# A fused attention and gated feed-forward kernel: idle matmuls at the start, kept products ahead of a rotary sum, and a split last projection

## What is computed

```python
xn = _layernorm(x, axis=-1)
# attention
q, k, v = xn @ wq, xn @ wk, xn @ wv          # heads of 128
q, k = _rope(q, pos), _rope(k, pos)
scores = einsum('bqhgd,bshd->bhgqs', qg, k) * sm_scale
allowed = (j <= i) & (j > i - SLIDING_WINDOW)
attn = softmax(where(allowed, scores, neg), axis=-1)
s = einsum('bhgqs,bshd->bqhgd', attn, v).reshape(...) @ wo
# feed-forward, W1, W2, W3 dequantised from 4 bits with a scale per 64
h = silu(xn @ W1.T) * (xn @ W3.T)
g = _silu(h @ W2.T)
x = x + s * g
```

## Time and profile before

| what | value |
|---|---|
| median of 3 runs | 816.35 us (815.01 to 816.83) |
| the profiled execution, its own time | 816.31 us |
| its span | 814.5 us |
| TensorE (PE) busy | 799.0 us, 98% of the span |
| VectorE (DVE) busy | 564.8 us, 69% |
| ScalarE (ACT) busy | 428.2 us, 53% |
| GpSimd (POOL) busy | 484.3 us, 59% |
| TensorE in the chain that ended last | 75% |
| GpSimd in the chain that ended last | 15% |

### The profile page before, as it was taken

How to read it: one execution, slowest core, us unless ns; L and a number is a source line. 1 busy time by engine, 2 the same in 40 slices (tenths; PEclk the granted TensorE clock), 3 DMA queues, 4 the chain that set the end, 5 groups by cost and what they waited for, 6 DMA issues and landing times.

```text
span 814.5 us, 13389 instructions
## 1 busy us (share of the span) xinstructions
PE 799.0 (98%) x3928; PEld 668.5 (82%) x3928; DVE 564.8 (69%) x1628; ACT 428.2 (53%) x1103; POOL 484.3 (59%) x362
## 2 busy tenths in 40 slices
PE   6999999999999999999999999999999999999987
PEld 4888888888888888888888888888888888888876
DVE  6625858576558867767686777768677676867774
ACT  4412313223138675666656576665656666665562
POOL 2112324224156774877488497747839774789985
PEclk9999999999999999999999999999999999999999
DMA  9449525211000400400030040003004001220102
GB/s 286 147 164 271 157 78 139 82 39 52 0 28 14 130 14 0 131 1 14 12 118 13 0 129 0 13 28 101 13 0 129 0 13 38 91 64 0 39 1 104
DMA packets 51908, 54.00 MB, mean 66 GB/s; under 512 B 4128, under 2 KB 33184, under 8 KB 51872
## 3 DMA queue, kind: packets, MB, share of 16 engines
q1 hardware_dynamic: 51584, 53.49, 22.0%
q10 hardware_dynamic: 288, 0.07, 0.0%
HBM read 47.25 MB, written 6.29 MB: 66 GB/s over the span
## 4 chain that ended last, share of the span: by engine, by line
PE 75%; POOL 15%; issue 6%; DVE 1%; ACT 1%; DMA 0%; POOLq 0%; ACTq 0%; DVEq 0%
PE bank L1270 20%; PE bank L1271 20%; PE bank L1272 20%; POOL wol L398 5%; POOL swap L424 5%; PE bank L1384 2%; PE bank L1397 2%; PE bank L1311 2%; PE bank L1316 2%; PE bank L1322 2%; POOL q L428 2%; POOL pl L447 1%; POOL ph L447 1%; POOL acc L455 1%; PE bank L1414 1%
## 5 line engine op out<-in xcount | busy, mean ns | idle before, releaser
L424 POOL TENSOR_TENSOR swap<-swap,cst 128x512 f32<-128x512 f32 x80 | 108.4, 1355 | 39.6 <-ACT swap L665 39.6
L686 ACT ACTIVATE probs<-probs,nmx 128x128 f32<-128x128 f32 x256 | 100.0, 392 | 60.4 <-DVE nmx L1055 60.4
L1270 PE MATMUL bank<-xh,wih 128*128 128x512 f32 x320 | 128.9, 403 | 0.0
L1271 PE MATMUL bank<-xl,wih 128*128 128x512 f32 x320 | 125.2, 391 | 0.0
L1272 PE MATMUL bank<-xh,wil 128*128 128x512 f32 x320 | 125.0, 391 | 0.0
L1270 PE MATMUL bank<-woh,oh 128*128 128x512 f32 x256 | 100.5, 392 | 0.1
L1271 PE MATMUL bank<-wol,oh 128*128 128x512 f32 x256 | 100.2, 391 | 0.0
L1272 PE MATMUL bank<-woh,ol 128*128 128x512 f32 x256 | 99.9, 390 | 0.0
L374 POOL TENSOR_TENSOR hl<-act_h,hh 128x512 fp32r<-128x512 f32 x22 | 32.0, 1454 | 102.2 <-ACT hh L564 102.2
L428 POOL TENSOR_TENSOR q<-q,swap 128x512 f32<-128x512 f32 x64 | 85.5, 1335 | 6.7 <-DVE q L1030 1.8
L447 POOL TENSOR_TENSOR ph<-ph,cst 128x512 fp32r<-128x512 f32 x32 | 42.8, 1338 | 72.0 <-ACT ph L701 72.0
(11 more groups left out here) (121 smaller groups left out, 2006.5 us busy)
## 6 DMA issues: line engine op xcount, KB each, us to landing
raw<-in_wq SPq DMA_DIRECT2D x32, 256.0 KB, 5.0
raw<-in_wo SPq DMA_DIRECT2D x32, 256.0 KB, 4.9
pk<-in_w SPq DMA_DIRECT2D x44, 128.0 KB, 3.7
sc<-in_s SPq DMA_DIRECT2D x44, 128.0 KB, 3.9
vals<-stage SPq DMA_DIRECT2D x16, 256.0 KB, 2.5
vraw<-vals SPq DMA_DIRECT2D x16, 256.0 KB, 3.0
pk<-in_w SPq DMA_DIRECT2D x11, 256.0 KB, 2.7
sc<-in_s SPq DMA_DIRECT2D x11, 256.0 KB, 3.0
```

The lines of the kernel that those rows point to most:

```text
L424: nc.gpsimd.tensor_tensor(v, v, spread(sin.unsqueeze(1), P, 2, SEQ), ALU.mult).then_inc(sin_done, 1)
L686: e = nc.scalar.activation(probs[:, s, c0:c1], probs[:, s, c0:c1], ACT.Exp, bias=nmx[:, s, i:i + 1], scale=-1.0, accum_out=rsum[:, s, i:i ...
L1270: nc.tensor.matmul(out_, sh, mh, start=(i == 0), stop=False)
L1271: nc.tensor.matmul(out_, sh, ml, start=False, stop=False)
```

## The change

1. **Start, TensorE.** `keep_busy(13)`: 13 matmuls on a zeroed tile `idle` (set by GpSimd) run ahead of the wait for the identity and the first turn; `keep_busy(2)` follows the first turn. Their bank is not read.
2. **Start, value units.** Of the waits in `v_unit` only those that can still be open are kept. Unit 0 does its four low-token matmuls ahead of the turn of tile 1, which stood between the first and the second four; with half 0 the low weights are taken in the order 0, 1, 3, 2.
3. **Start, GpSimd and VectorE.** GpSimd makes five chunks of `wvl` and VectorE three; GpSimd's waits are now on `ln_small` 6 and 12, the end of the small steps of tiles 0 and 1, and no longer on the normalised tiles.
4. **Feed-forward.** W2 tile 9 is handled beside tile 9 and no longer beside tile 10 (`W2_AT`), on all three engines. The first scores wait for the reading of token tile 7 alone; the wait for tile 6 stands ahead of the second scores.
5. **Attention steps.** On GpSimd `sin_part` is cut into product and sum, and the kept products of block 1 stand between product and sum of chunk 3. On ScalarE `p_hi(…, 1, 1)` stands ahead of `kq_hi(…, 2)`, and on VectorE `p_lo(…, 1, 1)` ahead of `kq_lo(…, 2)`.
6. **Last group.** `rest_product` 4 and 5 move from between the rotary parts to behind them.
7. **End.** The last out-projection is 24 matmuls of 256 columns, first the left half of the columns into O_B[1], then the right half into S_B[0], each with its own count; `finish_last` takes the halves as they come.

```diff
+        W2_AT = [()] + [(t - 1,) for t in range(1, FT - 2)] + [(FT - 3, FT - 2), (FT - 1,)]
...
-            pool.wait_ge(xn_here, 1)
-            wv_lo(0)
-            pool.wait_ge(xn_here, 2)
-            wv_lo(1)
-            wv_lo(2)
+            nc.gpsimd.memset(idle[:, :], 0.0).then_inc(idle_set, 1)
+            pool.wait_ge(ln_small, 6)
+            wv_lo(0, 0)
+            wv_lo(0, 1)
+            pool.wait_ge(ln_small, 12)
+            wv_lo(0, 2)
+            wv_lo(1, 0)
+            wv_lo(1, 1)
...
-                if last:
-                    rest_product(4)
                 sin_part(ng, nbp, 1)
-                if last:
-                    rest_product(5)
                 sin_part(ng, nbp, 2)
-                sin_part(ng, nbp, 3)
+                sin_product(ng, nbp, 3)
                 near(g, bp, 1)
+                sin_sum(ng, nbp, 3)
                 sin_part(ng, nbp, 4)
                 if last:
-                    rest_product(6)
-                    rest_product(7)
+                    for t in range(4, NT):
+                        rest_product(t)
                     for t in range(4, NT):
                         rest_sum(t)
...
                 p_hi(g, bp, 1, 0)
+                p_hi(g, bp, 1, 1)
                 kq_hi(ng, nbp, 2)
-                p_hi(g, bp, 1, 1)
                 halves(ng, nbp, 4)
                 kq_hi(ng, nbp, 3)
                 o_hi(g, bp, 2)
...
-                pe.wait_ge(xh_done, i + 1)
+                if half == 0:
+                    pe.wait_ge(xh_done, i + 1)
                 for d in range(DT):
-                    pe.wait_ge(wvh_done, DT * half + d + 1)
+                    if n in (0, 2):
+                        pe.wait_ge(wvh_done, DT * half + d + 1)
                     nc.tensor.matmul(out_, xh[:, d, cols], wvh[:, half, d, :], start=(d == 0), stop=False)
-                if ahead:
+                if ahead and n:
                     ahead()
...
+                if ahead and not n:
+                    ahead()
+                for d in ((0, 1, 3, 2) if half == 0 else range(DT)):
...
+            def keep_busy(n):
+
+                for _ in range(n):
+                    nc.tensor.matmul(bank[5][:, 0:P], idle[:, :], idle[:, :], start=True, stop=True)
...
+            pe.wait_ge(idle_set, 1)
+            keep_busy(13)
             pe.wait_ge(id_in, 16)
             x_turn(0)
+            keep_busy(2)
...
+            def last_project():
+
+                pe.wait_ge(ol_done, cnt(4, NKV - 1, 1, 4))
+                pe.wait_ge(acc_done, cnt(4, NKV - 1, 1, 2))
+                pe.wait_ge(masked, cnt(8, NKV - 1, 1, 7))
+                for half in range(2):
+                    cols = slice(half * D // 2, (half + 1) * D // 2)
+                    three(last_bank[half][:, cols], [(oh[:, 3, h, :], ol[:, 3, h, :], woh[:, h, cols], wol[:, h, cols])
+                                                 for h in range(GH)]).then_inc(y_ps, 1)
```

More of the change, by code:

```diff
@@ L94, in build @@
         warm = sb("warm", [P, 4], f32, ffn)
+        idle = sb("idle", [P, P], f32, ffn)
         stat = sb("stat", [P, NT, 6], f32, ffn)
@@ L186, in build @@
         PARTS = ((0,), (1,), (2, 3), (4, 5, 6, 7))
+        FIRST_LOW = ((0, 0), (0, 1), (0, 2), (1, 0), (1, 1))
+        THEN_LOW = ((0, 3), (1, 2), (1, 3))
         HERE = (0, 1, 2, 4, 6)
@@ L410, in _ @@
                 hid_lo(t, 0)
[L411 to L414, removed]
+                for u in W2_AT[t]:
+                    w2_lo(u)
                 hid_lo(t, 1)
@@ L428, in sin_part @@
                 nc.gpsimd.tensor_tensor(dst, dst, swap[:, s, :], ALU.add).then_inc(rope_done, 1)
+            def sin_part(g, bp, c):
+                sin_product(g, bp, c)
+                sin_sum(g, bp, c)
             pool.wait_ge(const_in, 16)
@@ L641, in _ @@
                         act.wait_ge(v_kept[i], 16 * (VU // 4))
[L642 to L645, removed]
+                for u in W2_AT[t]:
+                    w2_hi(u)
                 silu(t, 1)
@@ L967, in _ @@
             x_lo(1)
-            for d in range(DT):
-                wv_lo(1, d)
+            wv_lo(1, 2)
+            wv_lo(1, 3)
             stats(2)
@@ L1005, in _ @@
                     dequant13(t + 2, 1)
[L1006 to L1009, removed]
+                for u in W2_AT[t]:
+                    dequant2(u)
                 hid(t, 1)
@@ L1113, in finish_last @@
                 n = NT - 1
-                dve.wait_ge(y_ps, cnt(4, NKV - 1, 1, 4))
                 dve.wait_ge(rest_done, NT)
                 for half in range(2):
+                    dve.wait_ge(y_ps, cnt(4, NKV - 1, 1, 4 + half))
                     cols = slice(half * D // 2, (half + 1) * D // 2)
-                    nc.vector.tensor_tensor(gate[:, n, cols], O_B[1][:, cols], gate[:, n, cols], ALU.mult) \
+                    nc.vector.tensor_tensor(gate[:, n, cols], last_bank[half][:, cols], gate[:, n, cols], ALU.mult) \
                         .then_inc(acc_done, 1)
@@ L1222, in step @@
                 p_lo(g, bp, 1, 0)
+                p_lo(g, bp, 1, 1)
                 kq_lo(ng, nbp, 2)
-                p_lo(g, bp, 1, 1)
                 masking(ng, nbp, 0, 0, 1)
@@ L1307, in v_unit @@
                 out_, cols = bank[2 + n % 4][:, :], slice(i * P, (i + 1) * P)
-                pe.wait_ge(xh_done, i + 1)
+                if half == 0:
+                    pe.wait_ge(xh_done, i + 1)
                 for d in range(DT):
-                    pe.wait_ge(wvh_done, DT * half + d + 1)
+                    if n in (0, 2):
+                        pe.wait_ge(wvh_done, DT * half + d + 1)
                     nc.tensor.matmul(out_, xh[:, d, cols], wvh[:, half, d, :], start=(d == 0), stop=False)
-                if ahead:
+                if ahead and n:
                     ahead()
-                pe.wait_ge(xl_done, i + 1)
+                if half == 0:
+                    pe.wait_ge(xl_done, i + 1)
                 for d in range(DT):
                     nc.tensor.matmul(out_, xl[:, d, cols], wvh[:, half, d, :], start=False, stop=False)
[L1317 to L1322, removed]
+                if ahead and not n:
+                    ahead()
+                for d in ((0, 1, 3, 2) if half == 0 else range(DT)):
+                    if n in (0, 2) and (half, d) in FIRST_LOW:
+                        pe.wait_ge(wvl_first, FIRST_LOW.index((half, d)) + 1)
+                    elif n in (0, 2):
+                        pe.wait_ge(wvl_done, THEN_LOW.index((half, d)) + 1)
+                    m = nc.tensor.matmul(out_, xh[:, d, cols], wvl[:, half, d, :], start=False,
+                                         stop=(d == (3 if half else 2)))
                 m.then_inc(vu_ps, 1)
+            def keep_busy(n):
+                for _ in range(n):
+                    nc.tensor.matmul(bank[5][:, 0:P], idle[:, :], idle[:, :], start=True, stop=True)
             def w13_tile(t):
@@ L1450, in _ @@
             w2_mult(FT // 2, (0,), (7, 6, 4))
+            pe.wait_ge(ffn_read, place(FT // 2, 7))
+            scores(0, 0, 0, 0)
             pe.wait_ge(ffn_read, place(FT // 2, 6))
-            scores(0, 0, 0, 0)
             scores(0, 0, 0, 1)
@@ L1496, in step @@
                     out_project(g, bp, 2)
-                    out_project(g, bp, 3)
+                    last_project()
                     return
```

18 lines of the change are left out of this document (11 added, 7 removed).

## The result

The changed kernel takes **839.63 us** (median; 837.79 to 840.53, 4 runs) where the kernel before takes 816.59 (815.01 to 817.72, 4 runs) beside it: ratio 1.0279, 95% interval 1.0259 to 1.0299. It is slower, as forecast, but by 23 us and not by 16, and 0.6 us above the range of 825 to 839. The profiled execution took 840.53 with a span of 838.7.

What follows compares the result with a forecast made beforehand. TensorE, busy 799.0 of 814.5 us, was taken as the bound. Terms 21.8 - 2.3 - 2.2 - 0.3 - 0.3 - 0.6 = +16.1 us on 816.31 gave 832.4 us, range 825 to 839.

Steps and rivals of the forecast that it cites:

- The chain: Full attention steps: sum 4 behind both kept products delays `kq_hi`, `o_hi`, `o_lo`; TensorE's `out_project` 1 at 6.93, not 5.03.
- The sum of the gaps: 13 full steps: 1.90 us each in seven with bp=1, 1.41 in six with bp=0, together +21.8 us.
- the first step of the last group: Rest products behind the rotary parts shorten its 9.30 us distance to some 7.6; -2.3 us in all, bounds 0 and -4.5.
- the 0.6 for `finish`: Last group: VectorE's `finish` ahead of `p_lo` delays the chain by about 0.6, so 6.93 becomes some 7.6.
- Start, W2 and first scores: Unit 1 starts at 11.9, not 14.06 (-2.2); the `W2l` wait goes (-0.3); first scores wait for tile 7 alone (-0.3).
- The end: Last projection in halves: only one half's product and sum follow TensorE; -0.6 us, bounds 0 and -0.9.
- Rival 1: Whole kernel gets faster, because the held `o_hi` does not hold TensorE; about 806 us, chance 0.09.
- Rival 3: Gap smaller: GpSimd or ScalarE runs its chain part tighter, or only one step kind pays; 821 us, chance 0.07.
- rival 2: Attention steps: the clock falls at every new gap; chance 0.05.
- the part on what would show it: Signs in the profile: 13 `ol` waits of about 1.9 us, distance 6.9, unit 1 near 11.9, granted clock 1.00 through the steps.
- behind the gap their distances stay as they are: Attention steps: other engines shift along with TensorE, so the gaps add up in full and nothing more is lost.
- `p_hi` and `p_lo` earlier: Block 1 of attention steps: `ph` starts no earlier, and `kq_hi` of chunk 2 comes 0.6 us later; effect nothing.

Runs made afterwards that it cites:

- experiment 1: Changed kernel with ScalarE's `kq_hi` of chunk 3 moved behind the two `o_hi` of the step: 813.32 us, against 816.34 for the kernel before.
- Experiment 3: Kernel before with only GpSimd's kept products put between product and sum of chunk 3: 838.42 us, ratio 1.0269 to the kernel before.
- the kernel with the gap filled: Changed kernel with 8 unread matmuls of 512 columns ahead of `out_project` 1 in every full step: 834.37 us.
- experiment 6: Changed kernel with VectorE's list alone put back, `p_lo(…, 1, 1)` behind `kq_lo` of chunk 2: 850.78 us.

## Where the prediction was wrong, and where it was right

The step that failed is a term that I put at nothing: the falls of the clock behind the new gaps. The runs show 5.3 us in its place, and two smaller costs, of 1.4 and 0.7 us, that were not in the sum either. The chain that makes the gaps was right.

**Right: the mechanism and its place.** The chain turn, `ph`, two kept products, sum, `kq_hi`, `o_hi`, `o_lo` is what the trace shows, and experiment 1 cuts it at the link named. The steps of the working, from the turn: kept product 1.32 (1.31 measured), sum 3.82 (4.00), `kq_hi` 5.15 (5.32), `o_hi` 5.47 (5.64), `o_lo` 6.09 (6.25), TensorE 6.93 (7.00). The 0.18 lost at `pl` is partly given back by a shorter handover at the end. The sum of the gaps was +21.8 and is +22.5 (13.7 + 8.8), the 0.7.

**Right in size, partly by luck:** the first step of the last group, -2.3. Its distance alone gives 2.3, since it is 7.0 and not 7.6 (the 0.6 for `finish` did not come), and the last step has 0.45 more, where the kernel before still ran at the low clock (0.50 in 780.00 to 781.00, 0.77 in the next microsecond). The -2.3 has a 0.6 in it for matmuls at the low clock; no run shows that term by itself, and the trace of before shows 0.75 in its place: the matmul at L1423 takes 0.80 and the one of `out_project` 1 0.63, against 0.50 and 0.40 in the earlier trace rows, and from the one to the other it is 1.66 us (778.63 to 780.29) against 0.91 (634.14 to 635.05). Start, W2 and first scores were -2.8 together (-3.1 in the trace); unit 1 at 11.97 against the forecast 11.9 is a lucky hit, since eight other traces with this start have 12.22 to 12.82, and the start alone measured 1.3. The end, -0.6 (-0.65 in the trace, not resolved by itself). Rival 1, the faster one, needed the sum to be no hindrance; it is excluded. Rival 3 is excluded too.

**Wrong, and the step that failed: rival 2 was priced as all or nothing.** I wrote of the clock falling "at every new gap", gave it 0.05, and put nothing of it into the forecast, with the ground that each new gap stands alone, while ahead of the 0.52 of the earlier trace rows three stood close together. In the trace of before these are the 0.49 of the earlier trace rows and

```profile
775.73 0.47 PE L1414 MATMUL bank<-ph,vh 128*128 128x512 f32 x1 [1.15 <-DVE pl L1077]
...
777.39 0.51 PE L1420 MATMUL bank<-ph,vh 128*128 128x512 f32 x1 [0.73 <-POOL ph L447]
```

The new gaps do stand alone (those that end at 617.91 and 655.15 are 37 us apart), and the clock fell behind four of the 14 all the same, at 1.57 us each. The low stretch of the earlier trace rows had cost 1.3: the 0.75 above and 0.53 from `out_project` 1 to `out_project` 2 (4.45 us, where the step of the earlier trace rows has 3.92). So a price was at hand, a little low, and the count was wrong. By the kernel with the gap filled it is 5.3 us of the 7.2 between forecast and result. The granted clock was not at 1.00 through the steps, as the part on what would show it had expected. The rival's own sign of being right, a clock near 0.5 in windows behind the gaps, came at four of them.

**Wrong: "behind the gap their distances stay as they are".** After a wait the second matmul comes 0.11 later than in a running row (0.34 against 0.23): +1.4 over 14 stretches, in the fourth row of the table. One of the 14 lies behind `first_step`, where the same loss follows a hold of only 0.18 us at the weight load.

**Wrong: `p_hi` and `p_lo` earlier cost "nothing".** They move VectorE's `ql` into the start of GpSimd's `pl`. I had this as an upper bound of the gap, 2.3, but not as a cost of this edit. Experiment 3 puts it at 0.17 to 0.19 each step; it is inside the 7.00, where shorter handovers hide most of it.

Without the falls the forecast of 832.4 stands against 834.4 measured: 1.4 behind the waits and 0.7 in the gaps.

**Wrong: the upper end of the range.** By the bounds that I gave, 832.4 + 5.2 + 2.5 is 840.1, and I wrote 839. The result lies below 840.1, but this would have been luck: that room was meant for slower kept products, and the falls filled it.

**Open:** why the clock falls behind some gaps and not behind others of the same length. The earlier W2 tile, the first scores' wait and the rest products were seen in the traces but not run by themselves.

## What to carry to other kernels

When an instruction moves back on one in-order engine, ask which instruction on the next engine waits for it, and what stands queued behind that one, though it needs nothing of it: here 0.15 us of slack two engines further decided 29 us. A wait of 0.5 us in every other step was worth removing, but by filling idle time earlier on the late engine, not by overtaking something that others wait for. And price a new repeated gap in TensorE's row with a share of falls of the clock (here 4 behind 14 gaps of 1.8 us), with the cost of one taken from the trace (here 1.57 us), rather than with none or all.

## What the hardware did that I had not expected

**The clock falls behind single short gaps, sometimes.** Gaps of 1.8 us, one in about 37 us: 4 falls behind 14 in the profiled run, at clocks of 0.992 to 0.996 over the runs; with a hole of 0.9 in the same place none; with 1.62 to 1.63 in experiment 3 none in the 13 full steps of the one trace; with 1.82 in experiment 6 again 4 of 14. What tells the four from the ten these runs do not show.

**Of `pl` on GpSimd and `ql` on VectorE the one that started second took longer.** The kept product `pl` takes 1.48 us where it starts while `ql` runs, and 1.29 in experiments 3 and 6, where none runs at its start. `ql` takes 0.43 in a quiet place of experiment 1, 1.02 where it starts 0.56 us into `ph`, and 1.30 where it starts 0.26 us into `ph` (experiment 6); in both it ends 0.28 to 0.29 us after `ph` does. The product that was there first keeps its 1.28 to 1.30. In these rows it is not the overlap that counts but who came first.

**Faster first matmuls earn little by themselves.** The idle matmuls brought the first turn from 1.08 to 0.60 us for four, and the whole kernel nothing that can be measured, since the next limit, the low weights, lay right behind.
